# First stage of an adaptive feed-forward kernel: A's table in SBUF, another order of tiles, and the first pair's c kept in SBUF

## What is computed

```python
def _L0_cond_ref(x, adapter_mapping, W, b, lora_As, lora_Bs):
    base_out = jnp.einsum('bti,oi->bto', x, W) + b
    A = lora_As[adapter_mapping]           # 32 slots, [512, 16] each
    Bm = lora_Bs[adapter_mapping]          # 32 slots, [16, 512] each
    lora_h = jnp.einsum('bti,bir->btr', x, A)
    lora_out = jnp.einsum('btr,bro->bto', lora_h, Bm)
    return base_out + lora_out * SCALING   # SCALING = 2

def _L0_ffn_ref(x, W_gate, W_up, W_down):  # 512 -> 1376 -> 512
    up = jnp.einsum('td,fd->tf', xf, W_up)
    gate = jax.nn.silu(jnp.einsum('td,fd->tf', xf, W_gate))
    return jnp.einsum('tf,df->td', gate * up, W_down)

x = x + _L0_ffn_ref(_L0_cond_ref(x, itok_B_0_23, ...), ...)
x = x + _L1_ffn_ref(_L1_cond_ref(x, itok_B_0_7, ...), ...)   # second block, unchanged here
```

## Time and profile before

| | us |
|---|---|
| median of 3 runs | 978.82 (977.28 to 981.17) |
| profiled execution | 979.65 |
| its span | 977.9 |

### The profile page before, as it was taken

The page is one execution under the profiler, slowest core; times in us unless marked ns, Lnnn a source line. Parts: engine busy times, 40 slices in busy tenths (PEclk is TensorE's granted clock), DMA queues, the critical chain, the costliest instruction groups (busy, mean ns, idle before and its releaser), DMA issues.

```text
span 977.9 us, 14231 instructions
## 1 busy us (share of the span) xinstructions
PE 965.6 (99%) x4659; PEld 814.7 (83%) x4659; DVE 607.6 (62%) x1019; ACT 472.4 (48%) x877; POOL 264.8 (27%) x276
## 2 busy tenths in 40 slices
PE   8899999999999999999999999999999999999998
PEld 7788888888888888888888888888888899898986
DVE  5686797886992432795433398333378488786862
ACT  4666675665742333571333383233357274545342
POOL 5222344554301711400622130261140460000000
PEclk9999999999999999999999999999999999999999
DMA  7899877777979877877886777986688650616132
GB/s 235 293 347 306 261 266 286 262 287 251 352 239 319 280 195 194 279 244 254 287 268 194 235 239 258 320 279 195 193 283 302 237 195 22 237 42 217 65 108 87
DMA packets 131122, 230.14 MB, mean 235 GB/s; under 512 B 29797, under 2 KB 29798, under 8 KB 130538
## 3 DMA queue, kind: packets, MB, share of 16 engines
q1 hardware_dynamic: 126720, 216.35, 66.8%
q0 software_dynamic: 4192, 12.87, 3.6%
q10 hardware_dynamic: 138, 0.01, 0.0%
HBM read 165.74 MB, written 63.44 MB: 234 GB/s over the span
## 4 chain that ended last, share of the span: by engine, by line
PE 90%; DMA 3%; DVE 2%; SPq 1%; ACT 1%; issue 1%; ACTq 0%
PE bank L2084 90%; DMA c_scratch<-c_out 1%; SPq L636 1%; DMA wd_scratch<-dt 1%; PE bank L2254 1%; ACT c_out L1119 1%; DMA t_raw<-t_scratch 1%; DMA w_raw<-in_w 0%; DMA a_raw<-in_a_cols 0%; DVE ds L1687 0%; DVE dt L1632 0%; ACT dt L1145 0%; SPq L703 0%; SPq L622 0%; ACT cop_hi L1158 0%
## 5 line engine op out<-in xcount | busy, mean ns | idle before, releaser
L2084 PE MATMUL bank<-cop_hi,wring 128*128 128x512 f32 x1234 | 380.9, 389 | 0.9 <-ACT c_out L1119 0.7
L2084 PEld LDWEIGHTS bank<-cop_hi,wring 128*128 128x128 f32 x1234 | 231.7, 188 | 50.0 <-ACT c_out L1119 1.1
L2084 PE MATMUL bank<-cop_lo,wring 128*128 128x512 f32 x616 | 239.7, 389 | 0.0
L2084 PE MATMUL bank<-op_hi,wring 128*128 128x512 f32 x560 | 173.7, 389 | 0.0
L1695 DVE TENSOR_TENSOR v<-bank,p7s 128x512 f32<-128x512 f32 x44 | 30.4, 691 | 193.8 <-PE bank L2084 193.7
L2084 PEld LDWEIGHTS bank<-cop_lo,wring 128*128 128x128 f32 x616 | 115.7, 188 | 23.8
L2084 PEld LDWEIGHTS bank<-op_hi,wring 128*128 128x128 f32 x560 | 105.1, 188 | 21.8
L2084 PE MATMUL bank<-op_lo,wring 128*128 128x512 f32 x280 | 108.9, 389 | 0.0
L1219 ACT ACTIVATE s<-bank 128x512 f32<-128x512 f32 x44 | 26.3, 597 | 112.5 <-PE bank L2084 112.5
L2084 PE MATMUL bank<-xa,w_hi 128*128 128x512 f32 x256 | 76.3, 392 | 2.6 <-ACT c_out L1119 1.7
L1663 DVE TENSOR_TENSOR op_lo<-h,op_hi 128x512 fp32r<-128x512 f32 x100 | 72.6, 743 | 2.5 <-ACT op_hi L1176 2.3
(11 more groups left out here) (241 smaller groups left out, 1840.0 us busy)
## 6 DMA issues: line engine op xcount, KB each, us to landing
wring<-wgu_scratch SPq DMA_DIRECT2D x231, 256.0 KB, 3.0
wring<-wd_scratch SPq DMA_DIRECT2D x140, 256.0 KB, 5.4
wgu_scratch<-wring SPq DMA_DIRECT2D x77, 256.0 KB, 3.7
c_scratch<-c_out POOLq DMA_DIRECT2D x32, 256.0 KB, 3.8
c<-c_scratch SPq DMA_DIRECT2D x32, 256.0 KB, 3.1
xs_raw<-x_scratch SPq DMA_DIRECT2D x16, 512.0 KB, 6.2
out<-res SPq DMA_DIRECT2D x32, 256.0 KB, 2.1
x_raw<-in_x SPq DMA_DIRECT2D x14, 512.0 KB, 4.8
```

The lines of the kernel that those rows point to most:

```text
L2084: return e.matmul(out_ap, lhs, rhs, start=start, stop=stop, skip_group_check=True)
```

## The change

It has four parts, all in the first stage.

1. **A's table.** The whole table of A (32 slots, 8 KB in each partition, 1 MB) is loaded once into SBUF, `a_table`, which lies where `wring` 3 to 6 begin their use later. SP issues it after the third quarter of tile 1's x and before the fourth. GpSimd copies each sequence's piece from the table to `a_raw` with a register as address (`pick_a`, 16 copies of 128 x 64 a tile), after `gather` and ahead of its sums and its stores of c. SP's and GpSimd's small DMAs of A go, and SP issues the loads of x from tile 4 on one turn of its loop earlier.
2. **Order of tiles.** The tiles are worked in the order 2, 3, 4, 0, 1, 5, 6, 7 (`TILE_AT`). Below, "tile t" is the place in this order.
3. **c kept.** The pair 0, 1 (now in places 3 and 4) closes its c into SBUF: one half in c11 to c22, the other in `c_kept`, in parts of `cop_lo` that are written last. It is neither stored nor loaded; `cop_split` and `cop_rest` read it there. Half 0 of `cop_begin` waits for the closing only.
4. **Splits.** ACT's first `cop_split` waits for `dt_lo_done` and the fourth for down store 1; DVE's `cop_rest` of i = 1, 2, 3 waits for the store under it. `dt_` is laid out in another order for this. `cop_due` gives tiles 5, 6 and 7 4, 5 and 5 operands in place of 3, 4 and 7, and `cop_begin` of half 1 moves from tile 7 to tile 6.

```diff
+    dt_at = {i: work(f"dt{i}", [2, 2, 2 * P], F32R) for i in (1, 2, 3, 0)}
+    a_table = sb("a_table", [a_cols.shape[1], KC * R], F32, w_region + 3 * ROW)
+    kept_c = [((c11, c21), (c12, c22)),
+              tuple(tuple(sb(f"c_kept{2 * j + h}", [TOK], F32, cop_region + (7 * 2 * ROW) + (4 + 2 * j + h - 1) * 2 * ROW + ROW)
+                          for h in range(2)) for j in range(2))]
+    KEPT = (3, 4)
+    TILE_AT = list(range(2, 2 + KEPT[0])) + [0, 1] + list(range(2 + KEPT[0], NT))
...
-        first = {NT - 3: 0, NT - 2: 3, NT - 1: 7}
+        first = {NT - 3: 0, NT - 2: 4, NT - 1: 9}
...  SP
-            load_x(1, ks)
-        e.wait_ge(slot_list_in, DMA)
-        load_slots(0)
-        gather_a(0, (0,))
-        load_slots(1)
+            load_x(1, ks[:1])
+        e.dma_start(a_table[:, :, :], a_cols).then_inc(a_table_in, DMA)
+        load_x(1, [KC - 1])
...
-            for g in range(NG):
-                if 1 < t < NT - 2:
-                    load_x(t + 2, x_parts(t + 2)[g])
-                if t + 1 < NT:
-                    gather_a(t + 1, (g,))
+            if 1 <= t < NT - 3:
+                for ks in x_parts(t + 3):
+                    load_x(t + 3, ks)
...
-            if t == NT - 4:
-                load_c(0, 0)
             if t == NT - 1:
-                load_c(0, 1)
...  GpSimd
+        def pick_a(t):
+            for g in range(NG):
+                if t > 0:
+                    e.wait_ge(a_lo_done, NG * (t - 1) + g + 1)
+                for b in range(GB):
+                    slot = e.snap(slot_regs[g * GB + b], min_val=0, max_val=a_table.shape[1] - 1)
+                    e.tensor_copy(a_raw[:, g, a_place(b), :].unsqueeze(1), a_table[:, bass.ds(slot, 1), :]).then_inc(
+                        a_picked, 1)
...
         for t in range(NT):
             if t + 1 < NT:
+                load_slots(t + 1)
                 gather(t + 1)
+                pick_a(t + 1)
             if t in (NT - 3, NT - 2):
                 gate_up_sums(t - (NT - 3))
             for m in close_order(t):
-                e.wait_ge(c_closed, c_turn(t, m))
-                e.dma_start(c_dram[t, m], c_out[m][:, :]).then_inc(c_stored[m], DMA)
+                if t not in KEPT:
+                    e.wait_ge(c_closed, c_turn(t, m))
+                    e.dma_start(c_dram[TILE_AT[t], m], c_out[m][:, :]).then_inc(c_stored[m], DMA)
...  ACT
+                e.wait_ge(a_picked, GB * (NG * t + g + 1))
...
             if (s, q, i) == (0, 0, C_ORDER[0]):
-                for r in range(4):
-                    e.wait_ge(dt_stored[r], DMA * dt_stores(r, N_EARLY))
+                e.wait_ge(dt_lo_done, N_EARLY)
+            if (s, q, i) == (0, 0, 7):
+                e.wait_ge(dt_stored[1], DMA * dt_stores(1, N_EARLY))
...
-            if i in (1, 2, 3):
-                e.wait_ge(cst_in[{1: 0, 2: 2, 3: 3}[i]], DMA * (n + 1))
+            if i in (1, 2, 3) and s == 0:
+                e.wait_ge(c_closed, nth(KEPT[1]))
...  DVE
-            if t in (NT - 3, NT - 1):
-                cop_begin(0, (t - NT + 3) // 2)
             for q, i in cops[:3]:
+                if i == C_ORDER[0]:
+                    cop_begin(0, q)
                 cop_rest(0, q, i)
```

More of the change, by code:

```diff
@@ L113, in build @@
     ds = [work(f"ds{i}", [2, 2 * P], F32) for i in range(4)]
-    dt_ = [work(f"dt{i}", [2, 2, 2 * P], F32R) for i in range(4)]
+    dt_at = {i: work(f"dt{i}", [2, 2, 2 * P], F32R) for i in (1, 2, 3, 0)}
+    dt_ = [dt_at[i] for i in range(4)]
     within(cst_region, 5 * ROW)
@@ L342, in nth, with c_stores, c_place @@
         return t * KC + m + 1
+    KEPT = (3, 4)
+    TILE_AT = list(range(2, 2 + KEPT[0])) + [0, 1] + list(range(2 + KEPT[0], NT))
+    def c_stores(t):
+        return len([r for r in range(t) if r not in KEPT])
+    def c_place(t, m):
+        if t not in KEPT:
+            return c_out[m]
+        return kept_c[m % 2][KEPT.index(t)][m // 2]
     c_ring = [("h", t, g, "dve") for t in range(NT) for g in range(NG if t < 2 else 1)]
@@ L621, in load_x @@
             part = slice(ks[0], ks[-1] + 1)
[L622 to L637, removed]
+            e.dma_start(x_raw[t % 2][:, part, :], x[TILE_AT[t]][:, part, :]).then_inc(x_in[t % 2][ks[0]], DMA)
         def load_gate_up(j):
@@ L661, in load_c @@
             for m in range(KC):
-                e.wait_ge(c_stored[m], DMA * (2 * s + 2))
+                e.wait_ge(c_stored[m], DMA * c_stores(TILE_AT.index(2 * s + 1) + 1))
             e.dma_start(c11[:, :], c_dram[2 * s, q]).then_inc(cst_in[0], DMA)
@@ L1016, in pool_program @@
         e.dma_start(lang_i[:, :], lang_rows).then_inc(small_in, DMA)
+        e.wait_ge(slot_list_in, DMA)
+        load_slots(0)
+        e.wait_ge(a_table_in, DMA)
+        pick_a(0)
         for t in range(NT):
             if t + 1 < NT:
+                load_slots(t + 1)
                 gather(t + 1)
+                pick_a(t + 1)
             if t in (NT - 3, NT - 2):
@@ L1116, in close_c @@
             e.wait_ge(pe_acc, c_turn(t, m))
-            if t > 0:
-                e.wait_ge(c_stored[m], DMA * t)
-            e.activation(c_out[m][:, :], c_banks(t)[m][:, :], ACT.Identity, bias=b0_sb[:, m:m + 1]).then_inc(c_closed, 1)
+            if t not in KEPT and c_stores(t) > 0:
+                e.wait_ge(c_stored[m], DMA * c_stores(t))
+            e.activation(c_place(t, m)[:, :], c_banks(t)[m][:, :], ACT.Identity, bias=b0_sb[:, m:m + 1]).then_inc(c_closed, 1)
         def gate_up_hi(n):
@@ L1372, in act_program @@
                 close_c(t, m)
-                if t == NT - 1 and r == 1:
-                    cop_split(0, *cops[0])
-                    cops = cops[1:]
                 for n in d_due(t, r):
@@ L1636, in cop_begin @@
             n = 2 * s + q
-            for r in (0, 1, 3):
-                e.wait_ge(cst_in[r], DMA * (n + 1))
+            in11, in12, _, in22 = c_in(s, q)
+            if s == 0:
+                e.wait_ge(c_closed, nth(KEPT[1]))
+            else:
+                for r in (0, 1, 3):
+                    e.wait_ge(cst_in[r], DMA * (n - 1))
             if n > 0:
                 e.wait_ge(cop_lo_done, 7 * n)
-            e.tensor_tensor(c_t3[:, :], c22[:, :], c12[:, :], ALU.subtract).then_inc(c_t3_done, 1)
+            e.tensor_tensor(c_t3[:, :], in22[:, :], in12[:, :], ALU.subtract).then_inc(c_t3_done, 1)
             e.wait_ge(c_t3_done, n + 1)
-            e.tensor_tensor(c12[:, :], c12[:, :], c11[:, :], ALU.subtract).then_inc(c_t1_done, 1)
+            e.tensor_tensor(c12[:, :], in12[:, :], in11[:, :], ALU.subtract).then_inc(c_t1_done, 1)
         def cop_rest(s, q, i):
             n = 2 * s + q
+            _, _, in21, in22 = c_in(s, q)
+            if (s, q, i) == (0, 1, 7):
+                e.wait_ge(cop_lo_done, cop_n(s, q, 3))
+                e.wait_ge(c_t4_done, n + 1)
             e.wait_ge(cop_hi_done, cop_n(s, q, i))
-            e.tensor_tensor(cop_lo[i][:, q, :], cop_source[i][:, :], plain(cop_hi[i][:, q, :]),
+            if (s, q) == (0, 0) and i in (1, 2, 3):
+                under = {1: 2, 2: 3, 3: 0}[i]
+                e.wait_ge(dt_stored[under], DMA * dt_stores(under, N_EARLY))
+            e.tensor_tensor(cop_lo[i][:, q, :], cop_from(s, q, i)[:, :], plain(cop_hi[i][:, q, :]),
                             ALU.subtract).then_inc(cop_lo_done, 1)
@@ L1707, in product_1 @@
                 for m in range(KC):
-                    e.wait_ge(c_stored[m], DMA * NT)
+                    e.wait_ge(c_stored[m], DMA * c_stores(NT))
             dst = s1[0] if j == NF - 1 else (h11, h21)[j % 2][j // 2]
```

45 lines of the change are left out of this document (22 added, 23 removed).

## The result

| | before | after |
|---|---|---|
| median, us (11 runs each) | 978.27 (976.45 to 981.17) | 981.28 (978.59 to 982.53) |
| ratio after / before, 95% interval | | 1.0027 (1.0018 to 1.0037) |
| profiled execution, us | 979.65 | 981.28 |
| span, us | 977.9 | 979.2 |

A forecast was written before the change was run, and what follows sets the result against it. TensorE's first-stage gaps were taken as the bound: 7.0 us lost before, 4.8 after (1.8 + 0.2 + 0.3 + 2.5), a gain of 2.2 us, forecast 976.6 us. Range for 8 in 10: 972.7 to 983 us.

The forecast's parts named there:

- table lands: Tile 0: A's table, issued ahead of the last quarter of tile 1's x, is in SBUF at 17.2 us.
- a copy, alone: GpSimd's 128x64 copy from the table takes 0.30 us, between bounds of 0.14 and 0.585 us.
- tiles 0 and 1: First tiles: late table, shared PSUM bank and B's later DMAs cost TensorE 1.8 us.
- tile 2: Copies ready well ahead from tile 2 on, GpSimd's load 11.3 us against 15.7; gaps of tiles 2, 3, 5 go, 3.9 us.
- turns with the copies: DVE's two-input operations between h and lh_lo take turns with GpSimd's copies: 0.2 us lost for all tiles.
- gap by `c_out` in tile 5: TensorE's wait for the closing of c, counted at tile 6, goes through part 3: 1.87 us.
- tile 5 into 6: DVE has eight c operations in place of seven and TensorE comes earlier: 0.3 us lost, between 0 and 0.9.
- tile 6 into 7: Nine c operations on DVE beside GpSimd's four sums make tile 7's a_both late: 3.1 us, taken as 2.5.
- end of the stage: Last tile: with five splits in place of seven and no load of c, the 0.90 us gap goes.
- the premise: TensorE is full from 150 us, so a microsecond taken from its first-stage gaps moves the end by a microsecond.
- Rival 2: Copies lock DVE out in runs, tiles 2 to 6: 984 or 996 us; over 4.9 us slower, chance 0.10.
- the likeliest case: Whole kernel near the forecast, from 973.5 to 980.5 us; chance 0.56.

The follow-up runs named there:

- e1: Changed kernel with tiles 5, 6 and 7 given 3, 4 and 7 operands' splits again, c still kept: 976.84 us, ratio to before 0.9987.
- e2: Changed kernel with GpSimd's four sums of the second weight chunk one tile later: 977.43 us, ratio to before 0.9989.
- e4: Changed kernel with A fetched by 128 small DMAs as before, in place of table and copies: 980.01 us, ratio to before 1.0024.
- e3: Changed kernel with 14 spare matmuls on TensorE just before tile 7's a_both: 981.1 us, ratio to before 1.0033.
- e6: Changed kernel with splits 3, 4, 7 and tile 0's A by small DMAs ahead of the table's: 979.2 us, ratio to before 1.0006.
- e5: Kernel before with A's table and the copies alone (old order, c stored and loaded, splits 3, 4, 7): 978.81 us, ratio 1.0008.
- e9: Changed kernel with splits 3, 4, 7, slots loaded early, third chunk's sums held back, copies ahead of B's indirect DMAs from tile 2: 980.83 us.

## Why the prediction was wrong

**Step by step**, in us lost by TensorE (bracket + 0.16):

| step | forecast | profile after | verdict |
|---|---|---|---|
| table lands, us | 17.2 | 17.38 | right |
| a copy, alone | 0.30 | 0.23 | near |
| tiles 0 and 1 | 1.8 | 0.80 + 0.92 + 0.82 + 0.31 = 2.85 | low, but see the next row |
| first product starts, gain | 0 | 0.95 (6.23 to 5.28) | missed; net 1.9 |
| tile 2 | 0 | 1.12 | wrong |
| turns with the copies | 0.2 | 0 | right |
| gap by `c_out` in tile 5 | gone | gone | right |
| tile 5 into 6 | 0.3 | 0.83 | at its upper end |
| tile 6 into 7 | 2.5 | 3.63 | mis-sized |
| lower clock behind it | not in the sum | 1.64 | missed |
| end of the stage | gone | gone | right |

Lost after: 4.8 forecast, 10.1 measured. Against the 7.0 us of before and with the earlier start that is 10.1 - 7.0 - 0.95 = 2.1 us slower; the profiled span grew by 1.3, the medians by 3.0. The profiled execution of before lies 1.4 us over its median of 978.27, that of after on its own median; so 1.4 of the 3.0 us can't show between these two profiles. The 0.8 us between the sum and the span lie behind the first stage. Counted matmul by matmul, the changed kernel is 2.0 us behind at the first products of the second stage. There the kernel before loses another 0.4 us, in a pair that takes 0.99 us where the next take 0.62 (row below). From 150 to 941 us the distance is 1.6 to 1.5 us (the same eight matmuls stand at 941.21 before and at 942.69 after), and 1.3 at the end:

```profile
142.53 0.99 PE L2084 MATMUL bank<-cop_hi,wring 128*128 128x512 f32 x2
```

So the premise held here: the distance at 150 us is nearly that at the end.

**The step that failed** is part 4's term for tile 6 into 7: "I take 2.5 us, since the sums may start some ops later, behind the copies". The working had 3.1 us and cut it to 2.5; measured are 3.63 us, and 1.64 us of lower clock behind them, which stood in neither the sum nor the rivals. These two make 5.3 us where 2.5 were summed, and 2.8 us more than the forecast would by themselves have turned its gain of 2.2 us into a loss. e1 and e2 confirm it: one moves the work, the other the sums, and they get 4.1 and 3.8 us back.

For the gap itself the mechanism was right and the size wrong. The rows give the parts, in us ("due" is when TensorE could have started):

| kernel | first `cop_lo` | `a_both` | DVE between | `a_both` due | gap |
|---|---|---|---|---|---|
| forecast | 121.2 | | 7.1, with sums 9.9 | 128.75 | 3.1, taken as 2.5 |
| e2, no sums beside | 119.43 | 126.84 | 7.41 | 126.82 | 0.87 |
| e4, no copies | 118.36 | 127.36 | 9.00 | 125.90 | 2.31 |
| e3, spare matmuls | 119.07 | 128.74 | 9.67 | | |
| changed kernel | 119.23 | 129.22 | 9.99 | 126.44 | 3.63 |

The sums cost DVE 2.6 us in the changed kernel and 2.3 in e3, near the 2.8 read from the earlier trace rows. The sums do start 5.2 us later than in e4. But all four still end before DVE is at `a_both`, and DVE is never idle for more than 0.15 us from the first `cop_lo` on, so later was no relief. The other half microsecond is DVE's operations without sums (7.4 for 7.1) and TensorE, which wants `a_both` 7.2 us behind the first `cop_lo` in place of 7.55. That e4's gap comes near 2.5 us is luck: its sums cost 1.6 us, in a kernel without the copies for which the 2.5 was taken. Why they cost 1.6 there and 2.3 to 2.8 in the others stays open.

Rival 2, a lock-out by the copies, did not come. DVE was shut out by the sums: the operation of 2.30 us waited through the first two of them.

Of the rest, 1.1 us are tile 2 and 0.5 us tile 5 into 6. One slip is in the forecast's range: the lower bound of the likeliest case, 973.5 us, counts from the profiled 979.65; from the median, like the forecast, it is 972.6.

**Tile 2** was the second error. Its term held GpSimd's load against a whole tile (11.3 of 15.7 us) and found it well ahead. But GpSimd's list has the stores of tile 0's c ahead of it, which wait for ACT's closings and end at 36.24. The last copy is wanted at about 45.3, 1.4 us before TensorE is due at 46.7. That is 9.1 us and not 15.7, and slots, B and copies took 10.0, as the copies slow down beside DVE. Statistics of the copies' line (ns min/median/max), in tile 0 with DVE idle and in tile 6 with DVE full:

```profile
L1001 POOL COPY a_raw<-a_table x16: 227/229/695, 17.4 to 20.9; 128x64 f32 x16
...
L1001 POOL COPY a_raw<-a_table x16: 226/690/773, 115.6 to 123.6; 128x64 f32 x16
```

A copy beside DVE's 128x512 operation lasts as long as that operation, 0.69 us. The Trainium skill, "SBUF — State Buffer", section "Who interferes with whom", says that a DVE instruction with two SBUF inputs contends with a GpSimd instruction that reads SBUF and that who comes first holds the port for its whole instruction. By this rule, the trace agrees, it is the copies that wait, and I had used it in one direction only, to price DVE.

**Tiles 0 and 1**: group 0 and the shared bank cost 1.72 us, near the 1.65 forecast, but in part because TensorE had started 0.95 us earlier: tile 0's first `a_both` came at 20.40, 0.2 us sooner than before. Less that start the head lost 1.9 us, as forecast. In tile 1 the closing of c, behind B's late DMA, was not seen. It is the mechanism that e6 then made larger.

**Part 3** was right: ACT's three `cop_hi` start at 100.79 without a wait, and c is closed in time; e5, without it, still waits 2.11 us there. Tile 5 into 6 then lost 0.83 us as TensorE came earlier and the first chunk's sums fell beside `cop_lo` and `a_both` (DVE):

```profile
107.57 1.22 DVE L1678 TENSOR_TENSOR cop_lo<-c_t,cop_hi 128x512 fp32r<-128x512 f32 x1
108.72 2.49 DVE L1607 TENSOR_TENSOR a_both<-a_raw,a_both 128x256 fp32r<-128x256 f32 x4
```

**What stays open.** What the lower clock costs in this kernel's median was not separated from the gap (e3), nor what gives its time back there; why a third of the kernel before's runs have it too is not known, as its profile shows none. Why B's rows land as late as 31.79 us in e6 was not taken apart. Why the held operation waited for more than one GpSimd sum, 2.30 us, where its neighbours waited for one, was not tried; e3's profile holds another operation (1.85 us) for about the same total.

## What to carry to other kernels

When work is added to a queue, follow what stands behind it to where it now lands, and lower its price only if it lands beside idle time: here the copies held four sums back by 5 us, and DVE paid for them all the same. A forecast of a gap needs both sides' new times, since the engine that waits may come earlier too. Compare an engine's load with the window between its inputs' release and its outputs' use, not with the period of the loop, and apply a port rule to both engines. In the profiled executions four of five gaps of TensorE over 2 us were followed by lower clock, and none of the many under 2 us.

## What was not expected of the hardware

- The granted clock fell after four gaps, of 3.63 us (changed kernel), 2.3 us (e4), 2.97 us (e6) and 3.57 us (e9), and not after 2.27 us in e5 (by `c_out`, 106.86) or 1.87 us in the kernel before, all in profiled executions. At the lower level 22 matmuls took 4.91 us where 3.27 are usual.
- A register-addressed copy of 128x64 on GpSimd takes 0.23 us alone, in a pace of 0.23, and 0.69 us beside DVE's 128x512 operations with two SBUF inputs; loading 16 slots into registers holds GpSimd for 1.4 us (1.69 us idle ahead of the indirect DMA in place of 0.31).
- Of DVE's two-input operations beside GpSimd's 128x256 sums most took 0.3 to 0.6 us more. Single ones took 1.4 to 1.7 us more: 2.35 us in the earlier trace rows and 2.30 in the changed kernel where 0.7 are usual, 1.85 in e3 and 1.81 in e1 where 0.4 are. Beside 128x512 sums two weight splits took 2.94 us in place of 0.75, in e3 and in e2 alike.
